# A graph network's node stages: the last step of a group two steps behind its arrival in place of three, and the receivers' product ahead of the senders'

## The chip, the cores and the metric

The kernel runs on one core of one Trainium2 chip, as one program. Its engines work side by side: TensorE (PE in the rows), VectorE (DVE), ScalarE (ACT), GpSimd (POOL) and SyncE (SP), which only issues transfers. Each goes through its own list of instructions in order and waits for the others by semaphores. The metric is the device time of one execution in microseconds, lower is better.

## The reference

A graph with 6,250 nodes of 128 features and 106,250 edges, sorted by the receiving node (`dst`). Four graph layers follow on one another, each with a residual and a layer norm:

```python
edge_index = jnp.stack([src, dst])
x = _layernorm(x + _L0_gnn_ref(x, edge_weight, src, dst, W1, b1, W2, b2, U1, c1, U2, c2))
x = _layernorm(x + _L1_gnn_ref(x, factors, src, dst, Wm, bm, Wc, bc))
x = _layernorm(x + _L2_gnn_ref(x, edge_index, W, a_l, a_r))
x = _layernorm(x + _L3_gnn_ref(x, W_in, W_out, src, dst))
```

Layer 0 computes a message per edge from sender, receiver and edge weight, `relu(...) @ W1 ... @ W2`, takes the maximum over the edges of a node, and updates the node with `relu([x, agg] @ U1 + c1) @ U2 + c2`. Layer 1 sums `relu([x_src, factors_dst] @ Wm + bm)` and updates with `x + relu([x, agg] @ Wc + bc)`. Layer 2 is an attention over the edges with 4 heads. Layer 3 takes the mean of the senders twice: `relu(x @ W_in[0] + mean @ W_in[1])`, then the same with `W_out` and no ReLU. All in float32.

## The kernel before

The program is a row of stages: node stage 0, then for k = 1 to 5 a sweep over the edges and node stage k (the calls stand at the end of `gnn_program`). A **sweep** goes over 208 blocks of 512 edges: GpSimd gathers the rows of the senders, 128 at a time, by indirect transfers; TensorE turns them so that edges lie along the free dimension; VectorE scans along the edges with a running maximum or sum per receiver; TensorE turns the result back and it is stored row by row (`scan_rows`). The last row of each receiver holds its result.

A **node stage** (`node_phase`, L759) picks these rows and works on 13 groups of 512 nodes (four tiles of 128; the last group has one tile). For every group the engines do these steps, in this order:

- GpSimd `gather` (L796): four indirect transfers bring the group's rows into a ring of buffers. They are issued ahead of need.
- VectorE `aggregate` (L906): mask or mean (L930; in stage 1 L918 and L919), into `agg` (named `recv` in the rows).
- TensorE `turn_agg` (L1131, instruction L1135), ScalarE `keep_aggT` (L1053, L1058): the aggregate turned, out of PSUM.
- TensorE `product` (L1138, L1143 and L1144): the two halves of the first dense layer, ScalarE `hidden` (L1060, L1071 in stages 1 and 2): its ReLU.
- TensorE `product_rows` (L1146, L1153): the second layer, or a turn back, with nodes along partitions.
- VectorE `update` (L936): the residual (L949, L951, L959 or L962 in stages 1, 2, 4, 5), then the statistics of the layer norm (L968, L972). ScalarE `deviation` (L1074, L1078): the square root.
- VectorE `normalize` (L974, L984 and L986): the new x.
- TensorE `turn_x` (L1156, L1166), ScalarE `turned_x` (L1095, L1100): the new x turned.
- TensorE `tables` (L1169, L1180): up to two products of the new x for the next sweep, the senders' table (`w` in stage 0, `wh` in stage 2, PSUM bank 7) and the receivers' (`w` in bank 5, `wm` in bank 7, `w_score` in bank 3 in stages 0, 1 and 2). ScalarE `table` (L1107, L1116) and VectorE `receivers` (L1001; L1012 in stages 0 and 1, L1022 and L1023 in stage 2) copy them out. SyncE stores both (L845, L853), and GpSimd `scatter` (L816, L822) spreads the receivers' rows over the edges. When all are done GpSimd gathers a few first rows (L838), and the next sweep starts.

Stages 1, 2, 4 and 5 are `dense`, that is with products. Stage 3 has none, and stage 0 has only the last three of these steps (turned x, tables, receivers) and no gather. Stages 1, 2, 3 and 5 have the layer norm (`norm`), stages 0, 1 and 2 make a receivers' table. Stage 4's update is the copy of L959 and the store of the next sweep's table; stage 5 stores the result.

The order of each engine is written out by hand as a software pipeline: `straight` (L83) goes through steps i = 0, 1, 2, ..., and in step i it emits each piece of the engine's list for group i minus that piece's lag. The lags and their order within a step are in the lists `work` of each engine (L1031 for VectorE, L1120 for ScalarE, L1183 for TensorE, L826 for GpSimd). VectorE's step is: receivers, normalize, update, aggregate. TensorE's step is: tables, turn_x, product_rows, product, turn_agg. Two numbers set the lags of the later pieces: `late` (L778), the lag of update and deviation, and `new = late + norm` (L779), from which turn_x stands one step on, tables two, receivers three. The lags of product, hidden (1) and product_rows (2) are fixed.

Of the kernel before, what the change touches and what calls it, by code (L numbers as in the profile page):

```python
# [82 lines left out]
def straight(n, unroll, *pieces):  # L83


    for i in range(n + max(lag for lag, _ in pieces)):
        for lag, f in pieces:
            if 0 <= i - lag < n:
                f((i - lag) // unroll, (i - lag) % unroll)


def gnn_program(nc, a, out):
# [8 lines left out]
    def sem(name):  # L101
        return ctx.enter_context(nc.semaphore(name))
# [4 lines left out]
    with ctx:  # L107
# [103 lines left out]
        n_tab_ps = sem("n_tab_ps")  # L211
        n_recv_ps = sem("n_recv_ps")
# [546 lines left out]
        def node_phase(k):  # L759

            gathers = 1 <= k <= 5
            dense = k in (1, 2, 4, 5)
# [7 lines left out]
            w_tab = {0: w1[:, 0, :], 2: wh[:, :, :].rearrange("p k h -> p (k h)")}.get(k)  # L770
            w_recv = {0: w1[:, 1, :], 1: wm[:, 0, :], 2: w_score[:, :, :].rearrange("p m h -> p (m h)")}.get(k)
# [3 lines left out]
            to_w = F + HEADS if k == 2 else F  # L775
            agg_ps, hid_ps, rows_ps, x_ps, tab_ps = bank[0:2], bank[2], bank[4:6], bank[6], bank[7]
            recv_bank = {0: 5, 2: 3}.get(k, 7)
            late = 3 if dense else 1  # L778
            new = late + norm  # L779

            ring = spare if k == 1 else [gath[j] for j in range(NG)] if k == 3 else gath[RING:2 * STRETCH] if k >= 4 else gath[SLOTS:2 * STRETCH]
# [10 lines left out]
            def nodes(q, s):  # L792
                return slice(tiles(q, s).start * P, tiles(q, s).stop * P)
# [336 lines left out]
            def tensor(pe):  # L1130
                def turn_agg(q, s):  # L1131
                    pe.wait_ge(n_agg, 1)
                    pe.sem_inc(n_agg, -1)
                    for c in range(GROUP_TILES[2 * q + s]):
                        ins = pe.transpose(agg_ps[s][:, c * P:(c + 1) * P], agg[s][:, c, :], ident[:, :])  # L1135
                    ins.then_inc(n_agg_turned, 1)

                def product(q, s):  # L1138
                    n = GROUP_TILES[2 * q + s] * P

                    pe.wait_ge(n_aggT, 1)
                    pe.sem_inc(n_aggT, -1)
                    pe.matmul(hid_ps[:, 0:n], wa, aggT[s][:, 0:n], start=True, stop=False)  # L1143
                    pe.matmul(hid_ps[:, 0:n], wx, xT[:, nodes(q, s)], start=False, stop=True).then_inc(n_hid_ps, 1)  # L1144

                def product_rows(q, s):  # L1146
                    pe.wait_ge(n_hid, 1)
                    pe.sem_inc(n_hid, -1)

                    pe.wait_ge(n_rows_free, 1)  # L1150
                    pe.sem_inc(n_rows_free, -1)
                    for c in range(GROUP_TILES[2 * q + s]):
                        ins = pe.matmul(rows_ps[s][:, c * P:(c + 1) * P], hid[s][:, c * P:(c + 1) * P], back[:, :], start=True, stop=True)  # L1153
                    ins.then_inc(n_rows_ps, 1)

                def turn_x(q, s):  # L1156

                    if norm:

                        pe.wait_ge(n_x, 1)  # L1160
                        pe.sem_inc(n_x, -1)

                    pe.wait_ge(n_x_bank_free, 1)
                    pe.sem_inc(n_x_bank_free, -1)
                    for c in range(GROUP_TILES[2 * q + s]):
                        ins = pe.transpose(x_ps[:, c * P:(c + 1) * P], x_nm[:, (2 * q + s) * CT + c, :], ident[:, :])  # L1166
                    ins.then_inc(n_x_turned_a, 1)

                def tables(q, s):  # L1169
                    pe.wait_ge(n_xT_new, 1)  # L1170
                    pe.sem_inc(n_xT_new, -1)
                    for w, b, ready in ((w_tab, 7, n_tab_ps), (w_recv, recv_bank, n_recv_ps)):
                        if w is None:
                            continue

                        pe.wait_ge(n_bank_free[b], 1)
                        pe.sem_inc(n_bank_free[b], -1)
                        n = 2 * HEADS if b == 3 else F
                        for c in range(GROUP_TILES[2 * q + s]):
                            ins = pe.matmul(bank[b][:, c * n:(c + 1) * n], xT[:, nodes(q, s).start + c * P:nodes(q, s).start + (c + 1) * P], w, start=True, stop=True)  # L1180
                        ins.then_inc(ready, 1)

                work = ([(new + 2, tables)] * by_matmul + [(new + 1, turn_x)] * turn  # L1183
                        + [(2, product_rows), (1, product), (0, turn_agg)] * dense)
                straight(NG, 2, *work)
# [760 lines left out]
        def run(*programs):  # L1946

            with nc.Block() as block:
# [21 lines left out]
                def _(v):  # L1970
                    for gpsimd, sync, tensor, scalar, vector in programs:
                        vector(v)

        programs = [node_phase(0)]
        for k in range(1, 6):
            if k == 2:
                sweep = relation_phase()
            elif k == 3:
                sweep = attention_phase()
            elif k >= 4:  # L1980
                sweep = mean_phase(k)
            else:
                sweep = edge_phase(k)
            if k <= 3:
                started["firsts"] += TC
            programs += [sweep, node_phase(k)]
# [25 lines left out]
```

## Time and profile before

| what | value |
| --- | --- |
| median of 3 runs | 5549.13 us (5547.52 to 5549.64) |
| profiled execution | 5556.04 us |
| its span, first to last instruction | 5554.1 us |
| busy: TensorE, VectorE, ScalarE, GpSimd | 56%, 40%, 22%, 66% of the span |
| mean granted clock of TensorE | 0.71 of the full clock |
| instructions | 74,201 |

The node stages take only a small part of the span: stage 0 about 190 to 290 us, stage 1 about 1344 to 1485, stage 2 about 2034 to 2150, stage 4 about 4358 to 4430, and stage 5 from 5474 to the end. The rest is the five sweeps (and, at the start, the preparation of the indices). Times in the rows are us from the start of the span. Shares of the whole span say little about a node stage; it has to be read from the timeline of its own stretch.

### The profile page before, as it was taken

The numbers are of one execution on the slowest core, as the hardware profiler recorded it, in microseconds if no ns is written. First come the engines' busy times: TensorE is split into PE (matmuls) and PEld (weight loads), VectorE is DVE, ScalarE is ACT, GpSimd is POOL, SyncE is SP. The second block draws the span as 40 slices with busy tenths as digits, with TensorE's granted clock in tenths as the row PEclk, the third lists the DMA queues.
The fourth block names the chain that finished last, engine by engine and source line by source line (L and its number), as shares of the span: only waits on it lengthen the run. The fifth ranks groups of instructions, "written<-read, shape, count | busy, mean of one in ns | idle before, by whom it ended". The sixth has DMA issues, their size and how long they took to land. (4 is left out here: it accounts for less than half of the span.)

```text
span 5554.1 us, 74201 instructions
## 1 busy us (share of the span) xinstructions
PE 3095.5 (56%) x16332; PEld 2297.7 (41%) x16332; DVE 2246.7 (40%) x3963; ACT 1247.0 (22%) x2302; POOL 3646.4 (66%) x3815
## 2 busy tenths in 40 slices
PE   1488888887588884455554533333333433333335
PEld 1345555554477763444443423333333333333333
DVE  3134444444477763555554552222222222222224
ACT  0122222222244441222232231111111211111111
POOL 4377777776501127777777757777777677777776
PEclk7789999998799996777777765555555755555557
DMA  9789989897499983334343334444444344444443
GB/s 364 252 265 289 290 281 292 287 286 225 144 301 309 309 266 61 104 107 110 105 113 103 108 104 126 128 136 128 134 128 136 112 125 128 136 128 135 128 135 96
DMA packets 664991, 987.94 MB, mean 178 GB/s; under 512 B 143650, under 2 KB 366367, under 8 KB 654831
## 3 DMA queue, kind: packets, MB, share of 16 engines
q1 hardware_dynamic: 343332, 458.04, 25.2%
q0 software_dynamic: 134688, 301.60, 20.8%
q10 hardware_dynamic: 186804, 226.46, 11.3%
q8 instruction: 59, 0.97, 0.1%
q14 instruction: 108, 0.88, 0.0%
HBM read 553.21 MB, written 432.92 MB: 178 GB/s over the span
## 5 line engine op out<-in xcount | busy, mean ns | idle before, releaser
L1408 POOL DMA_INDIRECT gath<-sender_table,src_cols x1664 | 1573.8, 946 | 559.4 <-issue 503.1
L1448 PE MATMUL bank<-ident,gath 128*128 128x128 f32 x1664 | 463.4, 434 | 1283.6 <-DMA gath<-sender_table,src_cols 1283.6
L1675 POOL DMA_INDIRECT gath<-attention_table,src_cols x832 | 809.1, 973 | 253.7 <-issue 190.6
L1217 POOL DMA_INDIRECT gath<-joint_table,src_cols x832 | 791.9, 952 | 253.7 <-issue 191.2
L1448 PEld LDWEIGHTS bank<-ident,gath 128*128 128x128 f32 x1664 | 297.2, 217 | 1449.4 <-DMA gath<-sender_table,src_cols 1430.3
L1475 ACT ACTIVATE rows<-bank 128x512 f32<-128x512 f32 x416 | 248.5, 597 | 1855.1 <-PE bank L1458 1852.6
L813 POOL DMA_INDIRECT gath<-scan_rows,bounds_i x147 | 140.8, 958 | 559.1 <-issue 241.8
L1377 DVE TENSOR_TENSOR_SCAN scan<-meta,scan,bank 128x512 f32<-128x512 bf16 x208 | 266.2, 1280 | 446.0 <-DVEq L1374 437.0
L1492 DVE TENSOR_TENSOR_SCAN scan<-over_head,den,bank 128x512 f32<-128x512 bf16 x104 | 133.1, 1280 | 433.1 <-PE bank L1448 433.1
L1492 DVE TENSOR_TENSOR_SCAN den<-over_head,den,bank 128x512 f32<-128x512 bf16 x104 | 133.1, 1280 | 412.0 <-PE bank L1448 412.0
L1938 DVE TENSOR_TENSOR_SCAN scan<-bank,scan,hid 128x512 f32<-128x512 f32 x208 | 266.3, 1280 | 76.5 <-DVEq L1937 74.2
L1314 ACT ACTIVATE hid<-bank,b 128x512 f32<-128x512 f32 x208 | 143.0, 688 | 679.5 <-ACTq L1313 605.8
L1492 DVE TENSOR_TENSOR_SCAN den<-over_head,scan,bank 128x512 f32<-128x512 bf16 x104 | 133.1, 1280 | 398.7 <-PE bank L1448 398.7
L1273 PEld LDWEIGHTS bank<-same,recv 128*128 128x128 f32 x1664 | 223.3, 209 | 166.6 <-issue 166.6
L1640 DVE TENSOR_TENSOR_SCAN scan<-bank,scan,hid 128x512 f32<-128x512 f32 x208 | 265.9, 1278 | 25.8 <-DVEq L1639 25.7
L1273 PE MATMUL bank<-same,recv 128*128 128x128 f32 x1664 | 266.9, 309 | 0.0
L1492 DVE TENSOR_TENSOR_SCAN scan<-over_head,scan,bank 128x512 f32<-128x512 bf16 x104 | 133.1, 1280 | 323.7 <-PE bank L1448 323.7
L1363 DVE TENSOR_SCALAR same<-ahead,span_cols 128x128 f32<-128x128 f32 x832 | 187.9, 306 | 176.1 <-DVEq L1361 163.1
L1281 PE MATMUL bank<-hid,w 128*128 128x512 f32 x416 | 244.4, 673 | 0.3 <-ACTq L1316 0.3
L1271 PE MATMUL bank<-small,w1w 1*128 1x512 f32 x416 | 244.3, 668 | 0.0
L1760 PE MATMUL bank<-small,over_head 128*128 128x128 f32 x1664 | 241.7, 293 | 0.0
L1550 PE MATMUL bank<-ident,gath 128*128 128x128 f32 x832 | 238.9, 287 | 0.1
(282 smaller groups left out, 5886.3 us busy)
## 6 DMA issues: line engine op xcount, KB each, us to landing
scan_rows<-rows SPq DMA_DIRECT2D x624, 256.0 KB
recv<-receiver_rows SPq DMA_DIRECT2D x416, 256.0 KB
attention_scan_rows<-rows ACTq DMA_DIRECT2D x208, 264.0 KB
receiver_rows<-gath ACTq DMA_DIRECT2D x26, 2048.0 KB, 18.5
factor_rows<-gath ACTq DMA_DIRECT2D x208, 256.0 KB
scan_rows<-rows ACTq DMA_DIRECT2D x208, 256.0 KB
gath<-factor_rows SPq DMA_DIRECT2D x208, 256.0 KB
over_head<-edge_meta SPq DMA_DIRECT2D x52, 1024.0 KB
```

Source lines behind the costliest of these rows:

```text
L1217: pool.indirect_dma_start(out=landed[s][:, c, 0:width], out_offset=None, in_=table[:, :], in_offset=bass.IndirectOffsetOnAxis(ap=src_cols[ ...
L1271: pe.matmul(b[:, :], w1w[:, :], wrow[r][:, :], start=False, stop=False)
L1273: ins = pe.matmul(b[:, c * P:(c + 1) * P], recv[r][:, c, :], same[s % 2][:, c, :], start=False, stop=c == CT - 1)
L1281: pe.matmul(msg_ps[s % 2][:, :], w2[:, :], hid[s % 2][:, :], start=True, stop=True).then_inc(e_msg, 1)
L1377: chain(v.tensor_tensor_scan(scan[s % 2][:, :], go_on, src, scan[1 - s % 2][:, EB - 1:EB], ALU.add if expands else ALU.mult, ALU.max if ex ...
L1408: pool.indirect_dma_start(out=gath[s][:, c, 0:F], out_offset=None, in_=table[:, :], in_offset=bass.IndirectOffsetOnAxis(ap=src_cols[:, t:t ...
L1448: ins = pe.transpose(b[:, c * P:(c + 1) * P], gath[s][:, c, 0:F], ident[:, :])
L1475: act.activation(rows_flat[i % SLOTS][:, :, :], back_ps[i % DEEP][:, :].rearrange("p (c f) -> p c f", f=F), ACT.Copy).then_inc(e_rows, 1)
L1492: v.tensor_tensor_scan(sums[i % DEEP][:, :], go_on, pre_ps[i % DEEP][:, :], sums[(i - 1) % DEEP][:, EB - 1:EB], ALU.mult, ALU.add).then_in ...
L1640: chain(v.tensor_tensor_scan(scan[s % 2][:, :], go_ps[s % 2][:, :], hid[s % 2][:, :], scan[1 - s % 2][:, EB - 1:EB], ALU.mult, ALU.add))
L1675: pool.indirect_dma_start(out=gath[s][:, c, :], out_offset=None, in_=att_d[:, :], in_offset=bass.IndirectOffsetOnAxis(ap=src_cols[:, t:t + ...
L1938: chain(v.tensor_tensor_scan(scan[s % 2][:, :], fac_ps[s % 2][:, :], hid[s % 2][:, :], scan[1 - s % 2][:, EB - 1:EB], ALU.mult, ALU.add))
```

## The change

`late` becomes 2 in place of 3 in the dense stages. With it `new` and all lags that hang on it drop by one there: update and deviation stand two steps behind aggregate, normalize three, turn_x four, tables five, receivers six (in place of three, four, five, six and seven; the last four for stages with a layer norm). In `tables` the receivers' product is issued ahead of the senders'. This matters in stages 0 and 2, which have both.

```diff
             recv_bank = {0: 5, 2: 3}.get(k, 7)
-            late = 3 if dense else 1
+            late = 2 if dense else 1
             new = late + norm
...
                 def tables(q, s):
                     pe.wait_ge(n_xT_new, 1)
                     pe.sem_inc(n_xT_new, -1)
-                    for w, b, ready in ((w_tab, 7, n_tab_ps), (w_recv, recv_bank, n_recv_ps)):
+                    for w, b, ready in ((w_recv, recv_bank, n_recv_ps), (w_tab, 7, n_tab_ps)):
```

The orders of GpSimd and SyncE stay the same. VectorE at the start of stage 2, before and after (L1640 is the sweep's scan, L930 the aggregate, L951 the update, L968 its statistics):

```order
 L1640 SCALAR_TENSOR_TENSOR scan<-bank,scan,hid 128x512 x2
-L930 TENSOR_TENSOR recv<-gath,mask 128x512 x3
+L930 TENSOR_TENSOR recv<-gath,mask 128x512 x2
 L951 SCALAR_TENSOR_TENSOR recv<-x_nm,bank 128x512
 L968 BN_STATS stats<-recv 128x6 x4
```

Three aggregates stood ahead of the first update, now two do; the third stands behind it.

TensorE in stage 2, from the turned aggregate of one step to that of the next (L1135 turn_agg, L1180 the two tables, L1166 turn_x, L1153 product_rows, L1143 and L1144 product), the first such step with tables. Before:

```order
L1135 MATMUL bank<-ident,recv 128x128 x4
L1180 MATMUL bank<-wh,xT 128x128 x4
L1180 MATMUL bank<-w_score,xT 128x8 x4
L1166 MATMUL bank<-ident,x_nm 128x128 x4
L1153 MATMUL bank<-ident,hid 128x128 x4
L1143 MATMUL bank<-scan,wc 128x512
L1144 MATMUL bank<-xT,wc 128x512
```

After:

```order
L1135 MATMUL bank<-ident,recv 128x128 x4
L1180 MATMUL bank<-w_score,xT 128x8 x4
L1180 MATMUL bank<-wh,xT 128x128 x4
L1166 MATMUL bank<-ident,x_nm 128x128 x4
L1153 MATMUL bank<-ident,hid 128x128 x4
L1143 MATMUL bank<-scan,wc 128x512
L1144 MATMUL bank<-xT,wc 128x512
```

The two products of L1180 have changed places. What the rows can't show: the tables and the turned x in such a step belong to groups five and four steps back, before to six and five back. L1153 is of the group two steps back in both, and it is this group that VectorE now updates in the same step, where it took the one before.

On ScalarE the deviation of a group stood behind the hidden layer of the next but one; now it stands ahead of the hidden layer of the next (list `work` at L1120: deviation before hidden within a step).

## Rows read from the trace of the kernel before

**Rows 1.** Groups of instructions, GpSimd: names, shapes, count | busy us, mean ns | idle before.
```profile
L1217 POOL DMA_INDIRECT gath<-joint_table,src_cols x832 | 791.9, 952 | 253.7 <-issue 191.2 <-POOLq L1214 60.1 <-POOLq L1210 1.5
```
**Rows 2.** Window of stage 2: us, busy of each engine, PEclk, DMA share, GB/s.
```profile
2059.00:2101.00 42.00, 37.79 (x252) 29.08 (x252) 28.16 (x113) 18.47 (x34) 23.58 (x23) 1.00 0.44 113
```
**Rows 3.** Timeline of VectorE in stage 2: start, us, instruction, idle before it.
```profile
2058.18 0.66 DVE L930 TENSOR_TENSOR recv<-gath,mask 128x512 f32<-128x512 f32 x1
...
2088.15 0.66 DVE L930 TENSOR_TENSOR recv<-gath,mask 128x512 f32<-128x512 f32 x1
...
2089.51 0.16 DVE L1023 COPY score_o<-bank 128x16 f32<-128x16 f32 x1
...
2092.25 0.69 DVE L951 SCALAR_TENSOR_TENSOR recv<-x_nm,bank 128x512 f32<-128x512 f32 x1 [0.35 <-DVEq L946]
...
2094.49 0.66 DVE L930 TENSOR_TENSOR recv<-gath,mask 128x512 f32<-128x512 f32 x1
...
2112.59 0.17 DVE L1022 COPY rows<-bank 128x16 f32<-128x16 f32 x1
```
**Rows 4.** Timeline of TensorE in the same step of stage 2.
```profile
2089.11 0.63 PE L1135 MATMUL bank<-ident,recv 128*128 128x128 f32 x4 [0.86 <-PEq L1133]
2089.57 1.06 PE L1180 MATMUL bank<-wh,xT 128*128 128x128 f32 x8
...
2091.28 0.64 PE L1166 MATMUL bank<-ident,x_nm 128*128 128x128 f32 x4
2091.75 1.06 PE L1153 MATMUL bank<-ident,hid 128*128 128x128 f32 x8
```
**Rows 5.** Timeline, start of stage 2: TensorE's first product of rows, VectorE's first update.
```profile
2043.80 1.13 PE L1153 MATMUL bank<-ident,hid 128*128 128x128 f32 x8 [0.78 <-PEq L1151]
...
2045.08 0.69 DVE L951 SCALAR_TENSOR_TENSOR recv<-x_nm,bank 128x512 f32<-128x512 f32 x1 [6.05 <-DVEq L946]
```
**Rows 6.** Timeline of GpSimd, end of stage 2: first scatter of group 8, last scatter.
```profile
2114.09 0.97 POOL L822 DMA_INDIRECT receiver_score_rows<-score_o,bounds_i  x1 [0.47 <-issue]
...
2134.53 0.97 POOL L822 DMA_INDIRECT receiver_score_rows<-score_o,bounds_i  x1 [0.30 <-issue]
```
**Rows 7.** Timeline of stage 1: VectorE, then TensorE, then GpSimd's first scatter.
```profile
1382.31 0.69 DVE L1012 COPY same<-bank 128x512 f32<-128x512 f32 x1 [0.35 <-DVEq L1011]
...
1385.33 0.69 DVE L949 TENSOR_TENSOR recv<-x_nm,bank 128x512 f32<-128x512 f32 x1 [0.35 <-DVEq L946]
...
1389.42 0.69 DVE L1012 COPY same<-bank 128x512 f32<-128x512 f32 x1 [0.35 <-DVEq L1011]
...
1422.08 0.69 DVE L1012 COPY same<-bank 128x512 f32<-128x512 f32 x1 [3.55 <-DVEq L1011]
...
1383.30 1.13 PE L1180 MATMUL bank<-wm,xT 128*128 128x128 f32 x8 [0.41 <-PEq L1177]
...
1384.70 1.06 PE L1153 MATMUL bank<-u,hid 128*128 128x128 f32 x8
...
1390.41 2.05 PE L1180 MATMUL bank<-wm,xT 128*128 128x128 f32 x8 [0.41 <-PEq L1177]
...
1384.18 1.00 POOL L822 DMA_INDIRECT receiver_rows<-same,close_i  x1 [5.96 <-POOLq L819]
```
**Rows 8.** Timeline of stage 5: VectorE from its last wait, TensorE's last full product.
```profile
5517.27 0.69 DVE L930 TENSOR_TENSOR recv<-gath,inv_deg 128x512 f32<-128x512 f32 x1 [1.15 <-DMA gath<-scan_rows,bounds_i]
...
5522.35 0.66 DVE L930 TENSOR_TENSOR recv<-gath,inv_deg 128x512 f32<-128x512 f32 x1
...
5547.54 0.18 DVE L984 RECIPROCAL rstd<-std 128x4 f32<-128x4 f32 x1 [0.57 <-DVEq L979]
...
5538.91 1.13 PE L1153 MATMUL bank<-ident,hid 128*128 128x128 f32 x8 [0.56 <-PEq L1151]
```
**Rows 9.** Timeline of TensorE, end of stage 4: the last full group's product of rows.
```profile
4420.54 1.13 PE L1153 MATMUL bank<-ident,hid 128*128 128x128 f32 x8 [1.76 <-PEq L1151]
```
**Rows 10.** Timeline of stage 0: TensorE's first two products, VectorE's first copy.
```profile
196.21 3.39 PE L1180 MATMUL bank<-w,xT 128*128 128x128 f32 x16 [1.30 <-PEq L1177]
...
199.75 0.69 DVE L1012 COPY same<-bank 128x512 f32<-128x512 f32 x1 [32.92 <-DVEq L1011]
```

## The prediction

> **What bounds the kernel now.** Stages are named by k here: node stages 0 to 5, each but 0 behind a sweep over the edges. I read the groups of instructions first, then the windows, then the timeline of each engine inside the node stages. The costliest groups are GpSimd's gathers of single tiles, each about 950 ns and 0.3 us of issue behind the last: 832 of them are a sweep of some 1040 us [rows 1]. The sweeps stay as they are, and start when the node stage ahead has delivered. So the edit is worth what it does to the end of each node stage, 1 to 1; k=3 isn't touched.
>
> In stage 2, VectorE goes through its step without a real gap: from one aggregate (L930) to the next 6.34 us [rows 3]. Its short idle times are the same in every step and are the price of its own waits. TensorE runs its own step beside it and is ready early: it starts to turn the aggregate 0.30 us after VectorE ended it (2088.15 + 0.66 = 2088.81, to 2089.11), needs 0.46 us for it, 1.71 us for the two table products, 0.47 us for turning x, and 1.06 us for the product of rows, which ends at 2092.81 [rows 4]. The update at 2092.25 [rows 3] came before that: it used the product of the step before. That slack is what the edit removes. The granted clock is 1.00 there, the level of 2.4 GHz [rows 2].
>
> **The fill and the drain.** With the update two steps behind, one step less stands in each of the stages 1, 2, 4 and 5. It seems to save a step. It doesn't in stage 2: the update of group 0 starts 0.15 us after its product of rows ended (2043.80 + 1.13, to 2045.08) [rows 5]. That is set by turning, copying, product, ReLU and product, in that order, whatever the lag. Before, VectorE did three aggregates while it waited; now it can do two, and the third stands behind the update. From the update of group 0 to the receivers of group 0 it is four steps before and four steps after. So nothing comes earlier.
>
> **Stage 2, the new step.** The update of i-2 waits for the product of rows that TensorE computes in the same step i, behind the tables and the turned x, which stand behind the turned aggregate of i-1. VectorE and TensorE wait for each other in turn. From the end E of one aggregate: TensorE has turned it at E + 0.76. The receivers' product is first now, and its bank 3 is freed by L1023, which ends 0.86 us behind E (2089.51 + 0.16 against 2088.81) [rows 3]; TensorE starts 0.30 us after such a release (L1012 ends at 1383.00, L1180 starts at 1383.30) [rows 7]. So E + 1.16, plus 1.71, 0.47 and 1.06 is 4.40; plus 0.15 the update starts; from there to the end of the aggregate it is 2.90 us (2092.25 to 2095.15) [rows 3]. Sum: **7.45 us in place of 6.34**. With the old order of the two products the sum would be 7.05: 0.40 us of it belongs to the swap, which makes the long product queue behind the wait for bank 3.
>
> Steps: VectorE ended the aggregate of group 5 at 2058.84 (2058.18 + 0.66) [rows 3]. The changed order has aggregated only group 4 by then, and done the same updates, 0.2 us later (2059.05), since the loop with the turned x but no tables just binds. One step with tables but no receivers takes 7.05, seven more take 7.45, the last 0.4 us less for its single tile: E is at 2059.05 + 7.05 + 52.15 - 0.4 = 2117.85. The next update starts 4.55 us behind that and is done 2.3 us later, and the receivers of group 8 follow at once: 2124.7, where they were at 2112.59 [rows 3]. Before, GpSimd was just level with VectorE at this point: it started group 8's scatter at 2114.09 with 0.47 us of idle, and ran 16 scatters more with no wait until 2134.53: 1.28 us each, 5.1 per group [rows 6]. It can't make good what it gets late; its order and SyncE's are unchanged, both only start later. Stage 2: **+12.3 us at the full clock**. TensorE now waits about 2 of 7.45 us in a step. In stage 1 it waited a third of the time and had steps at the half clock, like the one with 2.05 us for eight matmuls instead of 1.13 [rows 7]; such a step costs the loop some 2.9 us. I allow for about half of one: **+14**, bounds +8 (all waits of TensorE half as long as I put them) and +21 (three slow steps).
>
> **Stage 1.** GpSimd waits 5.96 us for the first receivers, scatters from 1384.18, and then never waits [rows 7]. The stage is GpSimd's from there, so what counts is the start, and the tail. The start: four steps after an unmoved first update, of which VectorE alone sets three; the loop sets the one with tables. From one receivers' copy to the next the loop is: 0.99 us to L1180, 1.40 to L1153, 1.06, 0.15, and 4.09 from L949 to the next copy, together 7.69 where it was 7.11 [rows 7]. Working the four steps through gives +0.3 us, +2.4 if TensorE's table step falls into a half clock, as one did before just there. The tail: the receivers of group 5 waited 3.55 us for a scatter's landing (1422.08) [rows 7]. GpSimd then has two groups to scatter before it wants group 6, 10.5 us, and wants a copy 1.87 us ahead of its scatter (1382.31 to 1384.18): group 6 has 8.6 us, each further group 5.1 more. The loop gives 7.7, then 7.0 and 6.0 for the steps with a single tile and none: group 8 comes 1.6 us late at the full clock, some 4 with a slow step. **Stage 1: +4**, bounds 0 and +9.
>
> **Stage 4.** One group arrives about every 5.0 us, since its four gathers take GpSimd so long, and the product of rows for i-2 ends over a microsecond ahead of the arrival of i: the update moves into an idle time. The end is a chain: the last-but-one product of rows waits 1.76 us for ScalarE's ReLU [rows 9], with VectorE idle. A nearer update doesn't shorten it. **0**, bounds -0.5 and +0.5.
>
> **Stage 5.** Here is a gain. VectorE's step is 5.1 us (5517.27 to 5522.35), and it waits for gathers at the start and last at 5517.27, 1.15 us [rows 8]. At that moment it will have normalized and updated one group more, in time in which it had idled. From there it is busy to the end. The loop, with stage 2's terms but no tables and no x to turn, gives 0.15 + 2.90 + 0.30 + 0.46 + 1.06 = 4.9 us, just under that. The last full group's product of rows ends at 5540.04 (5538.91 + 1.13); its update starts at 5540.2, and with 2.3 us of update and statistics, 0.3 of deviation and the hand-overs L984 follows at 5543.1, where it is at 5547.54 [rows 8]. **-4.4**, bounds -4.7 and -1.5 (two slow steps behind 5517).
>
> **Stage 0.** Only the swap is felt. Both products of the first group took 3.39 us at the half clock, and the receivers' copy waits for the second of them [rows 10]; as the first of the two, it is ready 1.6 us sooner, and GpSimd's scatters, which bound this stage, start sooner. The senders' table comes later, which its store has room for. **-1.5**, bounds -1.7 and 0.
>
> ScalarE: the deviation of i-2 now stands ahead of the hidden layer of i-1, and waits for VectorE. The hidden layer is then done 0.35 us after E; TensorE wants it 3.3 us after E. Costed at nothing; without the tables (stage 5) its cover is some 0.1 us.
>
> **Sum:** -1.5 + 4 + 14 + 0 - 4.4 = +12.1 us. The profiled execution has a span of 5554.1 and took 5556.04 us, 6.9 more than the median of the runs; the differences are taken over to the median unchanged: 5549.13 + 12.1 = **5561**.
>
> **Rivals.**
> *A, the lag was idle depth (faster).* If the stage ended by the number of its steps, each would lose one: GpSimd's 5.96 us in stage 1, 6.3 in stage 2, 4.4 in stage 5, with the 1.5 of stage 0: -18, 5531. It decides if the first update isn't bound by its product of rows; but it is [rows 5]. 4%.
> *B, TensorE is not in the loop.* If it were ready before VectorE, as the order alone might suggest, stage 2 would cost the displaced aggregate, at most 0.9 us, stage 1 nothing: about -5, 5544. For it: modelled ends of matmuls. Against: the start of the update at 0.15 us behind such an end [rows 5]. 15%.
> *C, the clock.* In the loop every slow step of TensorE is on the path. If half of the steps of stages 1, 2 and 5 ran at 1.2 GHz, stage 2 would add another 12 us, stages 1 and 5 some 8: about 5581. For it: slow steps in stage 1, where TensorE waited a third of the time; against it: full clock in stage 2 [rows 2]. 14%.
> The Trainium skill, "TensorE: Matmul & The Clock Gate", section "HAM oscillation — how this bites in real kernels", speaks for C and against the change: waits in each turn of a loop can make the clock fall back each time, where denser work keeps it up. The trace has both kinds; by the rule alone the time would be 5581.
>
> **How the numbers follow.** My own case has 67%: its time, with the bounds above taken together, lies from 5550 to 5573. A measurement of this kernel can tell about 0.2%, 11 us, from no change, so the limit, 5560.2, runs through this case: two thirds of it are above. Slower: 0.44 and all of C, 0.58. Faster: A, 0.04. Same: 0.38. The range reaches into B and C: 5546 to 5578.
>
> **What would show it.** Stage 2: L930 to L930 about 7.4 us, an idle time of a microsecond ahead of L951 that ends with TensorE; the last scatter 12 us or more later behind the stage's start; wh behind w_score with a wait of 0.4 us ahead of w_score. Stage 1: no gain in GpSimd's first wait. Stage 5: the last normalization 4.4 us earlier. Stage 0: the first scatter 1.5 us earlier. Wrong if L930 to L930 stays at 6.3 (B), if the first receivers of stages 1 and 2 come about 6 us earlier (A), or if 2.05 us for eight matmuls is the rule in stage 2 (C).

## The result, and the profile after

| | before | changed |
|---|---|---|
| median of 5 runs each, us | 5547.52 | 5574.48 |
| ratio, 95% interval | | 1.0050 [1.0039, 1.0061] |
| span of the profiled execution, us | 5554.1 | 5569.4 |

The change costs 27 us, 0.5%. The two profiles are only 15.3 us apart: that of before stems from an execution 8.5 us above its median, that of the change from one 3.2 us below its own. So I compare stages, cut at GpSimd's rows: a sweep over the edges reaches from its first gather to the end of its last, a stage from there to the next sweep (stage 1 to the end of the last L838, stage 2 from the start of the last product of `ones_row`, stage 5 to the end of the span).

| stage | before, us | forecast | changed | changed again (e5) |
|---|---|---|---|---|
| 0 | 280.5 | -1.5 | +1.6 | +2.3 |
| 1 | 147.2 | +4 | +8.7 | +10.2 |
| 2 | 116.0 | +14 | +21.5 | +20.0 |
| 3 | 104.3 | 0 | -0.1 | -0.2 |
| 4 | 75.9 | 0 | -0.9 | -0.8 |
| 5 | 86.1 | -4.4 | -5.8 | -3.8 |
| sum | | +12.1 | +25.0 | +27.7 |

The five sweeps together are 9.7 us shorter in the changed kernel's profile (L1217 takes 948 ns on average where [rows 1] has 952), and 25.0 - 9.7 is the 15.3 us of the spans. The edit does not touch them, and they differ just so between profiles with the same lag (e2, with lag 3, has sweeps 7.9 us shorter than before).

VectorE in stage 2 of the changed kernel (start, us, instruction, idle before it), a slow step between two short ones:

```profile
2081.37 0.66 DVE L930 TENSOR_TENSOR recv<-gath,mask 128x512 f32<-128x512 f32 x1
...
2086.54 0.69 DVE L951 SCALAR_TENSOR_TENSOR recv<-x_nm,bank 128x512 f32<-128x512 f32 x1 [1.57 <-DVEq L946]
...
2088.78 0.66 DVE L930 TENSOR_TENSOR recv<-gath,mask 128x512 f32<-128x512 f32 x1
...
2095.96 0.69 DVE L951 SCALAR_TENSOR_TENSOR recv<-x_nm,bank 128x512 f32<-128x512 f32 x1 [3.07 <-DVEq L946]
...
2098.20 0.66 DVE L930 TENSOR_TENSOR recv<-gath,mask 128x512 f32<-128x512 f32 x1
...
2103.52 0.69 DVE L951 SCALAR_TENSOR_TENSOR recv<-x_nm,bank 128x512 f32<-128x512 f32 x1 [1.56 <-DVEq L946]
...
2105.76 0.66 DVE L930 TENSOR_TENSOR recv<-gath,mask 128x512 f32<-128x512 f32 x1
```

From L930 to L930 it is 7.41, 9.42 and 7.56 us, where it was 6.34 [rows 3]. The update's idle time of 0.35 us has become 1.57 or 3.07. TensorE in the slow step:

```profile
2089.74 0.63 PE L1135 MATMUL bank<-ident,recv 128*128 128x128 f32 x4 [1.62 <-PEq L1133]
2090.95 1.03 PE L1180 MATMUL bank<-w_score,xT 128*128 128x8 f32 x8 [0.59 <-PEq L1177]
2091.84 1.41 PE L1180 MATMUL bank<-wh,xT 128*128 128x128 f32 x8
2093.04 1.06 PE L1166 MATMUL bank<-ident,x_nm 128*128 128x128 f32 x4
2093.89 1.91 PE L1153 MATMUL bank<-ident,hid 128*128 128x128 f32 x8
```

It waits for the aggregate (1.62 us) and for bank 3 (0.59), and in the middle of the table products the clock falls: the turned x and the product of rows take 1.06 and 1.91 us, against 0.64 and 1.06 in [rows 4]. The product of rows ends at 2095.80, and the update starts 0.16 us behind it. Of eight steps in the loop three are so (9.03, 9.42 and 9.55 us). The granted clock, which has the two levels of 1.2 and 2.4 GHz, is 1.00 on average in the window of [rows 2]; here, with the falls in it, it is 0.92 (the number ahead of the DMA share):

```profile
2070.00:2131.00 61.00, 46.53 (x257) 34.84 (x255) 31.54 (x129) 19.72 (x38) 27.15 (x28) 0.92 0.25 59
```

In stage 1 every second step is slow. First VectorE's copies, then GpSimd's scatters that had to wait:

```profile
1390.49 0.69 DVE L1012 COPY same<-bank 128x512 f32<-128x512 f32 x1 [0.35 <-DVEq L1011]
...
1398.32 0.69 DVE L1012 COPY same<-bank 128x512 f32<-128x512 f32 x1 [0.49 <-DVEq L1011]
...
1407.78 0.69 DVE L1012 COPY same<-bank 128x512 f32<-128x512 f32 x1 [0.49 <-DVEq L1011]
...
1426.90 0.97 POOL L822 DMA_INDIRECT receiver_rows<-same,close_i  x1 [1.05 <-POOLq L819]
...
1436.43 1.03 POOL L822 DMA_INDIRECT receiver_rows<-same,close_i  x1 [4.74 <-issue]
...
1443.07 0.97 POOL L822 DMA_INDIRECT receiver_rows<-same,close_i  x1 [1.79 <-POOLq L819]
```

Copy to copy is 7.83 and 9.46 us; it was 7.11 [rows 7], and 7.25 to 7.38 in the next three steps. GpSimd, which never waited behind its first scatter, now does five times (1.11 and 1.13 us later on), 8.3 us beyond its usual 0.3.

### The profile page after: what moved, and what is told of

Its sections match the earlier page's. It is cut to its first block and busy times, and to the rows that moved or that the text cites. A ratio compares the mean times of both kernels' runs of the same rounds, so it can differ in the third digit from the quotient of the medians.

```text
span 5569.4 us, 74201 instructions
## 1 busy us (share of the span) xinstructions
PE 3102.8 (56%) x16332; PEld 2307.7 (41%) x16332; DVE 2247.2 (40%) x3963; ACT 1245.7 (22%) x2302; POOL 3635.3 (65%) x3815
## 3 DMA queue, kind: packets, MB, share of 16 engines
q10 hardware_dynamic: 186804, 226.46, 11.3%
## 5 line engine op out<-in xcount | busy, mean ns | idle before, releaser
L1217 POOL DMA_INDIRECT gath<-joint_table,src_cols x832 | 788.7, 948 | 253.5 <-issue 191.0
L1640 DVE TENSOR_TENSOR_SCAN scan<-bank,scan,hid 128x512 f32<-128x512 f32 x208 | 265.9, 1279 | 25.3 <-DVEq L1639 25.2
```

What stands on the lines that cost most here:

```text
L1217: pool.indirect_dma_start(out=landed[s][:, c, 0:width], out_offset=None, in_=table[:, :], in_offset=bass.IndirectOffsetOnAxis(ap=src_cols[ ...
L1640: chain(v.tensor_tensor_scan(scan[s % 2][:, :], go_ps[s % 2][:, :], hid[s % 2][:, :], scan[1 - s % 2][:, EB - 1:EB], ALU.mult, ALU.add))
```

## The experiments

The numbers behind a run are its median less that of the kernel before on the same chip, and the ratio. "Stage 2 +x" is against the table above.

**Lag alone (e1) and swap alone (e2).**

```
e1:  late = 2 if dense else 1
     for w, b, ready in ((w_tab, 7, n_tab_ps), (w_recv, recv_bank, n_recv_ps)):
e2:  late = 3 if dense else 1
     for w, b, ready in ((w_recv, recv_bank, n_recv_ps), (w_tab, 7, n_tab_ps)):
```

> The update two steps behind the arrival, the products in their old order (senders first). Theory: the cost is the loop VectorE-TensorE, in which tables and the turned x stand between an aggregate and the update; the swap adds only the wait of w_score behind bank 3, 0.2 to 0.6 us in each of eight steps of stage 2, and its shift of stage 0. So most of the +27 us stays: about +22 us against the kernel before (5570), stage 0 at its old length, stage 2 some 3 us shorter than in the changed kernel, with L930 to L930 at 7.05 us in fast steps and slow steps as before. Rival (the swap is the cost): within 5 us of the kernel before.

> The update three steps behind as before, the receivers' product first. Theory: nothing waits for TensorE in stage 2 with lag 3 (the product of rows is done 5.8 us ahead of its update), so stages 1 and 2 stay, and only stage 0 moves: first scatter 1.8 us earlier, end of the stage 1 to 2 us later. About +1.5 us against the kernel before, L930 to L930 6.34 us in stage 2. Rival (the swap carries the cost): +10 us or more, with stage 2 longer.

e1: +15.9 us, 1.0029 [1.0018, 1.0041]; stage 1 +9.2, stage 2 +12.7, stage 5 -4.7. That is 6 us less than I expected, because stage 2 lost its slow steps along with the swap. e2: +3.2 us, 1.0006 [0.9997, 1.0015]; no stage moved by more than 0.7, its first scatter came 2.4 us sooner (199.3 against 201.7) and its stage 0 still took 0.1 us more. The swap alone costs nothing that can be told; the lag is the cost, and with the lag the swap makes it dearer. Stage 2 of e1:

```profile
2072.89 0.63 PE L1135 MATMUL bank<-ident,recv 128*128 128x128 f32 x4 [1.62 <-PEq L1133]
2073.35 1.06 PE L1180 MATMUL bank<-wh,xT 128*128 128x128 f32 x8
2074.24 0.96 PE L1180 MATMUL bank<-w_score,xT 128*128 128x8 f32 x8
2075.06 0.63 PE L1166 MATMUL bank<-ident,x_nm 128*128 128x128 f32 x4
2075.53 1.06 PE L1153 MATMUL bank<-ident,hid 128*128 128x128 f32 x8
...
2079.93 0.63 PE L1135 MATMUL bank<-ident,recv 128*128 128x128 f32 x4 [1.63 <-PEq L1133]
```

The same 1.62 us ahead of the turn, no second wait, and 7.04 us a step, six times running at the full clock; only at the end of the loop stands one slow step, 9.7 us. Stage 1, where the swap changes nothing, has slow steps in e1 too: copy to copy 9.2 to 9.5 and 7.8 us by turns.

**Where the loop runs (e4).** The changed kernel, with TensorE's order altered:

```
-work = ([(new + 2, tables)] * by_matmul + [(new + 1, turn_x)] * turn
-        + [(2, product_rows), (1, product), (0, turn_agg)] * dense)
+work = ([(2, product_rows)] * dense + [(new + 2, tables)] * by_matmul + [(new + 1, turn_x)] * turn
+        + [(1, product), (0, turn_agg)] * dense)
```

> The changed kernel with one edit: in TensorE's step the product of rows stands ahead of the table products and the turned x. Theory (the loop runs through the tables): the product of rows ends 1.8 us behind the aggregate (turn 0.76, rows 1.06), at the half clock 2.9, both sooner than VectorE comes to its update (3.44 us); L930 to L930 in stage 2 goes back from 7.4 to 9.5 us to 6.34, stage 2 to within 2 us of its old length, stage 1 likewise; stage 5 keeps its 5 us. About -3 us against the kernel before (5545), range -7 to +3. Rival (another cause, such as the aggregate displaced behind the update, or the hidden layer behind the deviation on ScalarE): +10 us or more stays.

+3.6 us, 1.0005 [0.9996, 1.0014]; stage 1 +1.1, stage 2 +5.5, stage 5 -5.5. The range was -7 to +3 and stage 2 within 2 us, so this is somewhat dearer than forecast. VectorE and TensorE in its stage 2:

```profile
2079.88 0.66 DVE L930 TENSOR_TENSOR recv<-gath,mask 128x512 f32<-128x512 f32 x1
...
2084.34 0.69 DVE L951 SCALAR_TENSOR_TENSOR recv<-x_nm,bank 128x512 f32<-128x512 f32 x1 [0.35 <-DVEq L946]
```

```profile
2081.27 0.60 PE L1135 MATMUL bank<-ident,recv 128*128 128x128 f32 x4
2082.65 1.13 PE L1153 MATMUL bank<-ident,hid 128*128 128x128 f32 x8 [0.78 <-PEq L1151]
2083.61 0.96 PE L1180 MATMUL bank<-w_score,xT 128*128 128x8 f32 x8
```

With lag and swap both in place, the update is back at 0.35 us of idle and the steps with tables at 6.3 to 6.7 us. This settles what made the steps longer: the tables and the turned x between the aggregate and the product of rows. The aggregate displaced behind the update, and the deviation ahead of the hidden layer on ScalarE, are both still there, and the steps don't show them: the product of rows now waits 0.78 us for the ReLU, but is in time. What is left in stage 2 came at its end. The receivers of group 8 are copied 86.1 us into the stage (84.0 before), the last ones 107.5 (102.6): in these steps no aggregate is left, and the copies behind group 8's are 6.97, 5.88, 5.88 and 2.68 us apart, where they were 4.20, 5.20, 5.65 and 3.58. TensorE is at the half clock there (`wh` takes 2.05 us), but at the same place before as well. Why the end stretches was not tried further.

**What slows the steps (e5, e6, e7, e11).** e5 is the changed kernel again. The others add matmuls that change no value, in stages 1 and 2, ahead of the product:

```
 pe.sem_inc(n_aggT, -1)
+if k in (1, 2):
+    pe.matmul(hid_ps[:, 0:n], wa, aggT[s][:, 0:n], start=True, stop=False)
+    pe.matmul(hid_ps[:, 0:n], wx, xT[:, nodes(q, s)], start=False, stop=True)
```

That is e7. e6 has the first of the two alone, with stop=True; e11 has the condition `if k in (1, 2) and 3 <= 2 * q + s <= 10`.

> The changed kernel unaltered, as the mark for the three others on this chip and as a second trace of it. About +27 us against the kernel before. Theory (the slow steps come from the loop's own waits): stage 2 again has slow steps of 9.0 to 9.6 us between steps of 7.4 to 7.6, about 3 in 8, and in stage 1 every second step is near 9.5 us instead of 7.8; stage 2 about 21 us and stage 1 about 9 us longer than before. Rival (chance of one execution): slow steps at other places and in another number, stage 2 anywhere from +12 to +25.

> The changed kernel with one more matmul of 512 columns in stages 1 and 2: ahead of the product of the aggregate TensorE computes its first half once more into the same bank (0.86 us at the full clock), in the time in which it otherwise waits 1.6 us for the next aggregate. At a constant clock it costs nothing, as the hidden layer has over 3 us to spare. Theory (TensorE's waits in the loop let the clock fall, and a slow step costs the loop 1.6 to 2 us): half of the wait is filled, slow steps become rarer; +15 to +22 us against the kernel before, 5 to 12 less than the changed kernel. Rival (the clock does not follow the waits): the same as the changed kernel or slower by the longer slow steps.

> The same with both halves of the product computed once more (1.73 us at the full clock), which fills the whole wait of 1.6 us in stage 2. Theory: no slow step is left in the loops of stages 1 and 2, all steps of stage 2 are 7.5 to 7.7 us, of stage 1 7.8 to 8.0; the stages are 13 to 15 us (2) and 3 to 4 us (1) longer than before, in all +10 to +15 us against the kernel before. Rival: slow steps stay, and are longer by the 1.7 us that the added matmuls take at the half clock: +27 us or more.

> The changed kernel with both halves of the product computed once more as in e7, but only for groups 3 to 10, so that the start and the end of stages 1 and 2 have no added work. Theory: what is left is the loop at the full clock: receivers of group 0 as in the changed kernel (38 to 39 us into stage 2; 41.5 in e7), group 8's 59 to 60 us behind them (65.7 in the changed kernel); stage 2 about 14 to 16 us longer than before, stage 1 about 4, in all +13 to +17 us against the kernel before. Rival (e7's quiet clock was chance, or the added work pays only when it starts early): stage 2 again at +20 or more with slow steps.

e5: +28.4 us, 1.0055 [1.0041, 1.0068]; steps (L930 to L930) of 8.73, 9.05, 9.19 and 9.34 us alternate with 7.4 to 7.9 in stage 2, and in stage 1 copies 9.0 to 9.3 us apart stand among others of 7.8. The pattern belongs to the kernel. The first slow step of e5:

```profile
2068.11 0.63 PE L1135 MATMUL bank<-ident,recv 128*128 128x128 f32 x4 [1.63 <-PEq L1133]
2068.58 1.06 PE L1180 MATMUL bank<-w_score,xT 128*128 128x8 f32 x8
2069.49 2.05 PE L1180 MATMUL bank<-wh,xT 128*128 128x128 f32 x8
2071.33 1.06 PE L1166 MATMUL bank<-ident,x_nm 128*128 128x128 f32 x4
2072.19 1.31 PE L1153 MATMUL bank<-ident,hid 128*128 128x128 f32 x8
```

It has the wait of e1's steps and no second one, and yet the clock falls in it. So the wait for bank 3 doesn't explain each slow step. The swap also changes the order of the two products, and the one wasn't told apart from the other.

e6: +28.9, 1.0050 [1.0036, 1.0064], slow steps as before (9.55, 9.11 and 9.07 us): half a filling gives nothing, the forecast for it failed. TensorE waits only 0.5 to 1.4 us in a step there, less than the 1.62 us of e1, whose clock stays up for six steps. e7: +24.2, 1.0046 [1.0032, 1.0059]; not one slow step in the loops of stages 1 and 2. (One step of stage 1 takes 8.77 us, at the full clock: the copy that waits for a scatter's landing [rows 7] waits 1.44 us there instead of 0.49.) Stage 1's cost fell from +8.7 to +4.7. But stage 2 stayed at +20.2 and the whole above the +10 to +15 that I had expected. The added work also stands at the start, where the clock is low: the first update came 19.5 us into the stage, not 17.2. e11 leaves it out there: +17.8 us, 1.0032 [1.0020, 1.0045], stage 1 +2.6, stage 2 +16.9, just above the forecast of +13 to +17. Its clock stays up to the last step ahead of group 8's receivers, where there is no added work any more. Stage 2 of e7:

```profile
2082.30 1.02 PE L1145 MATMUL bank<-xT,wc 128*128 128x512 f32 x2
2083.16 1.02 PE L1146 MATMUL bank<-scan,wc 128*128 128x512 f32 x2
2084.02 1.02 PE L1147 MATMUL bank<-xT,wc 128*128 128x512 f32 x2
2084.95 0.63 PE L1135 MATMUL bank<-ident,recv 128*128 128x128 f32 x4
2086.16 1.03 PE L1183 MATMUL bank<-w_score,xT 128*128 128x8 f32 x8 [0.59 <-PEq L1180]
2087.05 1.14 PE L1183 MATMUL bank<-wh,xT 128*128 128x128 f32 x8
```

The wait of 0.59 us for bank 3 is still there, the one of 1.6 us is gone, and `wh` takes 1.14 us in place of 1.41. More work on TensorE makes this kernel 9 to 11 us faster than the changed one is (+17.8 against +27 and +28.4, each against the kernel before beside it; e5 and e11 ran on the same chip, and no run of e11 is as slow as the fastest of e5).

**Swap in stage 0 alone (e8)**, with lag 2 everywhere:

```
+ ((w_recv, ...), (w_tab, ...)) if k == 0 else ((w_tab, ...), (w_recv, ...))
```

> The update two steps behind, receivers' product first in stage 0 alone. Theory: stage 2 like the run with the lag alone, steps of 7.04 us at the full clock with few slow ones, 12 to 16 us longer than before; stage 0 within 1.5 us of its old length, since what the first scatter gains (1.8 us) is waited for behind the 4 MB clear; about +17 us against the kernel before. Rival (the swap costs in stage 0 and not in stage 2): +27 us, with slow steps in stage 2.

+21.3 us, 1.0035 [1.0021, 1.0049]; stage 2 +10.4, stage 0 +2.1. It was expected at +17. Stage 2 with the old order is +12.7 and +10.4 in two kernels, with the new one +21.5 and +20.0: there the swap costs 9 us.

**Late stages alone (e3: `late = 2` for k in (4, 5); e9: for k == 5; old order of products).**

> Lag 2 in stages 4 and 5 alone, lag 3 in stages 1 and 2, old order of the products. Theory: TensorE has no tables there, so the loop stays shorter than GpSimd's 5.1 us for a group; stage 5 ends about 5 us earlier behind its last gathers, stage 4 within 1 us. About -5 us against the kernel before (-0.1%). Rival (the lag costs in each dense stage): +5 us or more.

> Lag 2 in stage 5 alone, lag 3 in stages 1, 2 and 4, old order of the products. Theory: the only gain of the change is in stage 5, and stage 4 gives nothing; stage 5 is 4 to 5 us shorter, all other stages as before, about -4.5 us against the kernel before (-0.08%), which is below what can be told in the total and is read from the stage. Rival (stage 5's gain needs stage 4's edit, or is given back): stage 5 within 1 us of before.

e3: -3.7 us, 0.9994 [0.9985, 1.0003], stage 5 -4.4, stage 4 +1.6. e9: -1.7 us, 0.9998 [0.9989, 1.0007], stage 5 -5.4, stage 4 +0.8. In the total neither can be told from no change; in the stage the gain is in each of the eleven profiles with lag 2 in stage 5, from -2.6 to -5.8. Stage 4 lies between -0.9 and +2.1 with lag 2, between 0 and +0.8 with lag 3.

**Warm start (e10):** e9, and in `product`, ahead of its wait for the first group in stages 1 and 2:

```
+for c in range(10 if k == 1 else 6):
+    pe.matmul(hid_ps[:, 0:P], ident[:, :], ident[:, :], start=True, stop=True)
```

> The kernel of e9 with matmuls of ident into the free bank of the hidden layer, 10 in stage 1 and 6 in stage 2, while TensorE waits for the first copied aggregate. Theory: the first update of both stages hangs on a chain of products that runs at the half clock because TensorE waited 4 to 6 us before it (2.04 us for two matmuls that take 1.02 later); kept busy, the chain is 1.5 to 3 us shorter in each, and with it both stages: -7 to -10 us against the kernel before. Rival (the clock doesn't come back in time, or the chain is set by ScalarE): as e9, or slower by matmuls that aren't done when the aggregate is.

-5.6 us, 0.9988 [0.9979, 0.9997], short of the forecast of -7 to -10, but the only kernel whose interval lies wholly below 1. In stage 1 the clock was back in time, in stage 2 it wasn't (the first products of each):

```profile
1349.01 1.10 PE L1146 MATMUL bank<-scan,u 128*128 128x512 f32 x2 [0.56 <-PEq L1145]
...
2030.17 2.77 PE L1143 MATMUL bank<-ident 128*128 128x128 f32 x12
2033.78 2.05 PE L1146 MATMUL bank<-scan,wc 128*128 128x512 f32 x2 [0.84 <-PEq L1145]
```

Stage 1 is -2.7 (e9: -1.7), stage 2 +1.3 (e9: +0.9). Most of its gain is stage 5's (-4.2). Against e9, in runs beside it, its median is 3.9 us lower, but in the profiles stage 1 is only 1.1 us shorter than e9's and stage 2 0.4 us longer. So how much the warm start gives isn't shown.

## Why the prediction was half right

- **The cause was right.** Fill and drain save no step in stage 2: the first update starts 17.2 us into it, 16.5 before (16.4 to 17.2 with either lag, over all kernels without added work). VectorE and TensorE wait for each other in turn. Forecast were steps of 7.45 us, and 7.05 without the swap; measured are 7.41 to 7.56 where the clock stays up (7.9 in two of the eight steps of e7), and 7.04 in e1. Rival B (TensorE not in the loop) and A fall with that.
- **"I allow for about half of one" slow step is the term that failed.** From 12.3 at the full clock to 14, that allowance is 1.7 us. From group 0's receivers to group 8's it was 48.3 us before and is 65.7 in the changed kernel, 64.2 in e5. In e7, whose clock stays up, it is 59.5 (60.9 in e11, which has one slow step at its end). So the slow steps add 4.7 to 6.2 us, and the loop at the full clock adds 11.3, where the forecast has about 10. Start and end of the stage give the rest: group 0's receivers +2.6, where I had 2.2 (2059.05 + 7.05 + 0.46 against 2064.34), the last steps +1.0 and the last scatter behind them +0.5, where I had nothing.
- **A slow step costs less than 2.9 us:** 1.4 to 1.7 in both stages. Set beside the same step of e7, the changed kernel's 9.55 is 7.91 there, and e5's are 1.4 to 1.7 us longer in turn; in stage 1 it is 9.46 against 7.82. In the steps shown the clock falls only behind the turned aggregate and is back within the next product. Their number was the error, so rival C came true in part: three or four steps of eight, at little more than half of its price.
- **Stage 1: "+4, bounds 0 and +9".** At the full clock its terms give about +2 (0.3 at the start and 1.6 at the tail, which by the terms printed should be 1.9); measured are +2.6 (e11) and +4.7 (e7, with added work at the start too). With slow steps in turn it is +8.7 to +10.2, at the bound. The rows had shown one such step where TensorE waited a third of the time [rows 7], and I counted one instead of every second.
- **The swap was costed at 0.40 us a step**, some 3 us, and costs 9. Its own wait is as forecast (0.1 to 0.6 us), and so is what it costs at the full clock: group 0 to group 8 takes 59.5 us in e7 and 56.6 in e8. The rest is the slow steps that come with it in stage 2, where e1 and e8 have hardly any.
- **Stage 5: -4.4**, measured -5.8 and -3.8, right. **Stage 4: 0**, right within the 2 us that it scatters.
- **Stage 0: "-1.5" has the wrong sign.** The first scatter came 1.7 us sooner, as worked out. But later GpSimd waits for a copy of VectorE, and this for a store that stands behind the 4 MB clear of `scan_d` in SyncE's queue (so the order says; it wasn't tried). Before, it waited 4.93 us there and went on at 244.90; in the changed kernel:

```profile
246.23 0.97 POOL L822 DMA_INDIRECT receiver_rows<-same,close_i  x1 [7.22 <-POOLq L819]
```

  The gain is waited away there. Stage 0 is between 0 and +1.4 in the five profiles with the old order, -2.1 and +3.1 in the eight with the new: nothing that can be told.

The Trainium skill, "TensorE: Matmul & The Clock Gate", section "HAM oscillation — how this bites in real kernels", tells of a kernel in which each turn of a loop began at the low clock, behind a wait for a DMA longer than the waits here. The trace agrees in part: the clock falls in three or four of eight turns of stage 2, and in every second one of stage 1. It doesn't fall in six turns of stage 2 of e1, whose wait of 1.62 us is the same.

The range held the time, but not by the case that I had argued. My own case was to end at 5573, and 5574.48 lies above it; the upper bounds of its terms, added up, give +29, or 5578. The range reached that far only to take in rival C. The sum of +12.1 was less than half of the 27 us: most steps read off rows came out within 0.1 us, the term that was allowed for without rows did not. What makes the clock fall in one step and not in the next stays open.

## What to carry to other kernels

A software pipeline's lag is slack for the engine that isn't the bound. Before it is cut, write down the whole step of the partner engine in its order: what stands between its input and the output that is now wanted in the same step joins the loop. With the wanted product moved to the front of TensorE's step, +3.6 us were left of +27. And where a cut makes TensorE wait in each step, cost the loop at the low clock too: here up to every second step was slow, each by 1.4 to 1.7 us.

## What was not expected of the hardware

- A wait of 1.62 us in each step of 7.04 us left the clock at its full level for six steps running in stage 2 (e1, and e8 likewise). With the other order of the two products it fell in three or four steps of eight, one of them with no more waiting than in e1 (e5). Filling 0.86 us of the wait didn't help (e6), filling all of it did (e7: granted clock 0.99 over the window that has 0.92 in the changed kernel). The length of the wait alone doesn't tell when the clock falls.
- After a wait at the sweep's end, 4.47 us of matmuls brought the clock back for stage 1's first product (1.10 us in place of 2.05), 2.77 us of them did not in stage 2 (e10, one profile).
- A profile's sweeps differ by some 2 us each between executions, with the gathers' mean at 946 or 943 ns: more, over five sweeps, than most terms of this case. Stages cut at the bounding engine's rows were comparable where spans were not.
